# A graph network on one core: the scaled variance ahead of the second half's normalisation, and two buffers of powers

## The reference, cut to what matters

```
m_j = einsum('bnd,do->bno', h, W1[:D])
m_i = einsum('bnd,do->bno', h, W1[D:])
pre = m_j[:, None, :, :] + m_i[:, :, None, :] + b1
msg = gelu(_layernorm(pre, g1, be1), approximate=False)
agg = einsum('bijo,bij->bio', msg, adjacency)
updated = _layernorm(concatenate([h, agg]) @ W2 + b2, g2, be2)
```

## Time and profile before

| | |
|---|---|
| time, median of 3 runs | 4087.21 us (4080.77 to 4090.16) |
| the profiled execution | 4083.3 us, of which the span 4081.4 us |
| granted TensorE clock, mean | 0.923 |
| busy: DVE, PE, ACT, POOL | 83%, 81%, 68%, 52% of the span |
| slot steps | 310, in 16 groups |

### The profile page before, as it was taken

One profiled execution on the slowest core, in us unless ns is written; L12 is line 12 of the kernel. 1 busy time (PEld: TensorE's weight loads), 2 busy tenths in 40 slices (PEclk: granted clock), 3 DMA queues, 4 the chain that ended last, 5 costly groups with the idle time before them and its releaser, 6 DMA issues.

```text
span 4081.4 us, 93269 instructions
## 1 busy us (share of the span) xinstructions
PE 3302.0 (81%) x25274; PEld 2780.7 (68%) x25556; DVE 3378.2 (83%) x12271; ACT 2785.5 (68%) x6381; POOL 2108.6 (52%) x1923
## 2 busy tenths in 40 slices
PE   3484688887888888888798888888887887988898
PEld 2273567677676777767677776767776676776777
DVE  4788888898888888888888888888898888887830
ACT  2484676858667586776858676685868768595753
POOL 1182663718547292753729274471827547192730
PEclk7596899989899999999999999999999999999999
DMA  2000001000010100001010000101000010000000
GB/s 81 26 1 26 1 1 42 1 22 21 1 43 1 43 0 22 22 1 43 1 35 9 22 22 1 43 1 43 0 22 22 1 43 1 27 0 1 16 1 21
DMA packets 95513, 73.89 MB, mean 18 GB/s; under 512 B 7504, under 2 KB 95184, under 8 KB 95184
## 3 DMA queue, kind: packets, MB, share of 16 engines
q1 hardware_dynamic: 95184, 70.09, 5.7%
HBM read 61.68 MB, written 8.39 MB: 17 GB/s over the span
## 4 chain that ended last, share of the span: by engine, by line
issue 26%; POOL 25%; DVE 21%; PE 16%; ACT 6%; DVEq 3%; POOLq 2%; ACTq 0%; DMA 0%; SPq 0%
POOL v_z L511 18%; POOL v_diag L517 3%; PE n_bank_d L1599 3%; PE n_bank_d L1600 3%; PE n_bank_c L1582 3%; DVE v_normed L971 2%; PE n_bank_d L1596 2%; POOL v_prstd L525 2%; DVE v_top_at L1043 2%; PE n_bank_b L1660 1%; DVE v_top L1040 1%; PE n_bank_d L1496 1%; ACT v_pair L842 1%; DVE v_adj_x L1048 1%; POOLq L532 1%
## 5 line engine op out<-in xcount | busy, mean ns | idle before, releaser
L511 POOL TENSOR_TENSOR v_z<-v_z,all_bc_L_gnn_be 128x512 f32<-128x512 f32 x620 | 786.2, 1269 | 22.0 <-DVE v_z L1093 22.0
L525 POOL TENSOR_TENSOR v_prstd<-v_pvar,all_neg_half 128x8 f32<-128x8 f32 x310 | 563.5, 1818 | 267.8 <-DVE v_pvar L1109 240.0
L1496 PE MATMUL n_bank_d<-v_diag,v_msg 128*128 128x128 f32 x4960 | 637.1, 284 | 32.2 <-ACT v_diag L740 32.2
L1496 PEld LDWEIGHTS n_bank_d<-v_diag,v_msg 128*128 128x128 f32 x4960 | 594.8, 197 | 35.2 <-ACT v_diag L740 35.2
L740 ACT ACTIVATE v_diag<-all_ident,v_value 128x128 f32<-128x128 f32 x1860 | 572.5, 386 | 0.0
L1485 PE MATMUL n_bank_b<-v_parts,v_onehot 128*128 128x128 f16 x5472 | 374.0, 224 | 152.6 <-ACT n_bank_b L682 152.6
L1485 PEld LDWEIGHTS n_bank_b<-v_parts,v_onehot 128*128 128x128 f16 x5472 | 332.7, 100 | 224.7 <-ACT n_bank_b L682 183.5
L1582 PE MATMUL n_bank_c<-all_l_wsd,v_fT 128*128 128x256 f32 x1792 | 449.1, 392 | 31.4 <-ACT v_adjT L667 28.9
L1485 PE MATMUL n_bank_c<-v_parts,v_onehot 128*128 128x128 f16 x4960 | 346.9, 226 | 141.7 <-ACT n_bank_c L682 141.6
L1485 PEld LDWEIGHTS n_bank_c<-v_parts,v_onehot 128*128 128x128 f16 x4960 | 308.6, 101 | 213.2 <-ACT n_bank_c L682 168.4
L677 ACT ACTIVATE v_fT<-n_bank_d,all_l_c 128x256 f32<-128x256 f32 x256 | 119.7, 474 | 447.1 <-PE n_bank_d L1600 446.9
(11 more groups left out here) (281 smaller groups left out, 7344.6 us busy)
## 6 DMA issues: line engine op xcount, KB each, us to landing
v_adj_l<-in_adj SPq DMA_DIRECT2D x128, 256.0 KB, 3.7
v_adj_x<-in_adj SPq DMA_DIRECT2D x64, 256.0 KB, 3.4
v_ring<-in_x SPq DMA_DIRECT2D x16, 512.0 KB, 5.9
out_x<-v_xout SPq DMA_DIRECT2D x64, 128.0 KB, 2.0
w_wu<-in_L_gnn_wu SPq DMA_DIRECT2D x4, 192.0 KB, 2.5
all_W<-in_L_gnn_W SPq DMA_DIRECT2D x2, 128.0 KB, 4.3
w_raw<-in_L_gnn_ws SPq DMA_DIRECT2D x1, 192.0 KB, 3.0
w_raw<-in_L_gnn_wd SPq DMA_DIRECT2D x1, 192.0 KB, 3.1
```

Of the source, the lines that this page charges most:

```text
L511: nc.gpsimd.tensor_tensor(z[par][:, units], z[par][:, units], wide(bc["L2_gnn_be1"])[:, units], ALU.add).then_inc(sem["z_ready"], 1)
L525: nc.gpsimd.tensor_tensor(prstd[:], pvar[:], minus_half, ALU.pow).then_inc(sem["prstd_ready"], 1)
L1496: ins = nc.tensor.matmul(ps_agg[:, u // NB, (u % NB) * P:(u % NB + 1) * P], msg[par][:, u], diag[par][:, u], start=False, stop=False, skip ...
```

## The change

Two edits. DVE scales the variance (`pvar`) directly behind the statistics of the second half, and the second half's normalise comes behind it. The powers go to one of two buffers, by `par`, so that the next slot's powers may be written while those of the slot before are still read.

```
-        prstd = plan.sb("prstd", [P, UNITS])
+        prstd = plan.sb("prstd", [P, 2, UNITS])
...
-                    nc.gpsimd.tensor_tensor(prstd[:], pvar[:], minus_half, ALU.pow).then_inc(sem["prstd_ready"], 1)
+                    nc.gpsimd.tensor_tensor(prstd[:, par], pvar[:], minus_half, ALU.pow).then_inc(sem["prstd_ready"], 1)
...
-                        ins = v.scalar_tensor_tensor(z[par][:, u], ps_m[par][:, u], prstd[:, u:u + 1],
+                        ins = v.scalar_tensor_tensor(z[par][:, u], ps_m[par][:, u], prstd[:, par, u:u + 1],
...
                         ins.then_inc(sem["stats_done"], 1)
-                        if not first:
+                        if half_ == 0 and not first:
                             dve.wait_ge(sem["prstd_ready"], step + 1)
-                            dve.wait_ge(sem["msg_ready"], step * 2 + (half_ + 1))
-                            normalise(1 - par, half_)
+                            dve.wait_ge(sem["msg_ready"], step * 2 + 1)
+                            normalise(1 - par, 0)
                     dve.wait_ge(sem["stats_done"], step * 2 + 2)
                     v.tensor_scalar(pvar[:].rearrange("p (q u) -> p q u", u=2), pstats[:, par, :, :, 2], 1.0 / D, UP * UP * LN_EPS,
                                     ALU.mult, ALU.add).then_inc(sem["pvar_ready"], 1)
+                    if not first:
+                        dve.wait_ge(sem["msg_ready"], step * 2 + 2)
+                        normalise(1 - par, 1)
                     pick(dve.snap(step + g * 2 + 2), par)
```

## The result

The changed kernel takes 4122.7 us (median of 4, 4121.5 to 4123.9) against 4086.0 (4 runs, 4080.8 to 4090.2): ratio 1.009, 95% interval 1.0075 to 1.0105. Forecast were 4096 us and 4066 to 4112: a loss of 9 us, where it is 37.

What follows compares the result with a forecast made beforehand. POOL's own work and a loop through DVE's `pvar` were taken as tied at 5.11 us a step. The profiled 4083.3 us plus 16 x 0.6 = 9.6 gave 4093; from the median 4087.2, about 4096 us, range 4066 to 4112.

Steps and rivals of the forecast that it cites:

- parts (a) to (d): Steady step: `pvar` moves 1.03 us earlier, is held by POOL's shift; the loop through ScalarE gives 5.10 us, from 5.11.
- Three signs: `pvar` mean 0.7 to 0.9 us; powers 1.65 to 1.75 us; shift at a group's end waits about 0.6 us.
- part (e): Group's end, 16 times: later second-half normalise and gather make POOL's shift 0.6 us later; 9.6 us in all.
- the first steps: Start of a group: powers of step 3 come 0.05 to 0.1 us sooner, the last powers 0.2 us sooner.
- Rival 4: Slot phase: later gathers in first steps delay the 2.4 GHz clock, or a loop term grows; 13 to 16 us more; chance 0.12.
- it is 0.6 us later, and with it the next mix: Group's end: the late shift delays the next mix by as much, nothing covers it; 16 x 0.6 is 9.6 us.

Runs made afterwards that it cites:

- x5: Kernel before, its order kept, with `pvar` as a TENSOR_REDUCE instead of a TENSOR_SCALAR: 4071.6 us, ratio 0.9949.
- x6: Changed kernel with `pvar` as a TENSOR_REDUCE instead of a TENSOR_SCALAR: 4057.3 us, ratio 0.9906.
- x12: Changed kernel with TENSOR_REDUCE `pvar`, no wait for the last gather, matmuls of zeros in the mix and each group's second step: 3986.3 us, ratio 0.9741.
- x2: Kernel before, its order kept, with six unused normalisations ahead of a group's last eight to make its end late: 4129.4 us, ratio 1.009.
- x4: Changed kernel with ten matmuls of zeros in TensorE's 2.61 us wait in the mix: 4091.9 us, ratio 1.000.
- x3: Changed kernel without VectorE's wait for a group's last gather: 4118.5 us, ratio 1.0064.

## Why the prediction came out wrong

**Right: parts (a) to (d).** `pvar` arrives in the shift and is held to its end (0.68 us, ends 0.04 behind the shift); the powers don't hold DVE; the loop is that of the second-half normalise, ScalarE and the gather, and the step is 5.096 us over the later steps, 5.10 forecast. Of the 1.03 us moved 0.015 a step is kept. x5 and x6 show the hold by taking it away. Three signs were off in size: the mean of `pvar` is 0.62 us (0.7 to 0.9 forecast), the powers are recorded with 1.78 (1.65 to 1.75), and the shift at a group's end waits 1.11 for DVE (0.6). One reading was loose: the TENSOR_SCALAR at 342.89 ends 0.28 us behind POOL's instruction, not with it; nothing rests on the difference.

**Right in kind, 0.17 us short: part (e).** Forecast from powers to shift were 4.54 us (1997.32 to 2001.86), measured 4.71 in the group shown. The term that is off is the one from the last second-half normalise to its gather: 2.21 forecast, 2.39 measured. The row it came from has 2.24 (1996.07 to 1998.31), so 0.03 was lost there for no stated reason. The 0.15 left is ScalarE's: the last gather starts 1.98 us behind its first seed before and 1.97 after (1996.33 and 2008.57 for the seeds), but that seed now comes 0.42 behind the second-half normalise, as ScalarE is still at its gelu, where it was 0.26. The other two, 1.28 and 1.21, measured 1.28 and 1.20. As a mean over the groups the end grew by 0.92 (14.8 over 16), where it was to be 0.8.

**Wrong: the first steps.** With the fourth powers 0.05 to 0.1 us sooner, and the steps behind them, a group's last powers were to come 0.2 us sooner, 3.2 in all. Measured is 0.8 later in all (+1.9, -1.1). The first two steps do better than I had followed: 4.60 and 4.93, 0.65 less than before. The third gives 0.76 back. PE's timeline of these steps, with ScalarE's second seed of the second step, before and in the changed kernel:

```profile
1903.88 1.89 PE L1485 MATMUL n_bank_b<-v_parts,v_onehot 128*128 128x128 f16 x16 [3.00 <-ACT n_bank_b L682]
...
1909.79 1.89 PE L1485 MATMUL n_bank_c<-v_parts,v_onehot 128*128 128x128 f16 x16 [1.46 <-ACT n_bank_c L682]
...
1912.32 1.44 PE L1485 MATMUL n_bank_c<-v_parts,v_onehot 128*128 128x128 f16 x16
...
1904.92 0.60 ACT L682 ACTIVATE n_bank_b<-v_own 128x512 f32<-128x512 f32 x1 [1.09 <-DVE v_z L1093]
```

```profile
1914.48 1.07 PE L1488 MATMUL n_bank_b<-v_parts,v_onehot 128*128 128x128 f16 x16 [2.85 <-ACT n_bank_b L682]
...
1921.10 1.89 PE L1488 MATMUL n_bank_c<-v_parts,v_onehot 128*128 128x128 f16 x16 [3.14 <-ACT n_bank_c L682]
...
1923.63 1.91 PE L1488 MATMUL n_bank_c<-v_parts,v_onehot 128*128 128x128 f16 x16
...
1916.23 0.60 ACT L682 ACTIVATE n_bank_b<-v_own 128x512 f32<-128x512 f32 x1 [1.81 <-DVE v_z L1093]
```

The gathers into bank c start 10.50 us behind the group's first powers (1910.60), where before it was 9.79 (1900.00). These 0.71 us are the hold: ScalarE's second seed waits for the second-half normalise, which stands behind the held `pvar`, and follows the first seed by 2.41 us where it was 1.70. Every group has the shift of 0.7 us, and in x6, where nothing is held, it is 0.2. The clock comes on top. In the group shown the bank c gathers take 1.89 and 1.91 us at 1.2 GHz; before they took 1.89 and 1.44, so they were mostly at the low level too, while the gather of 1903.88 was at 1.2 GHz before and that of 1914.48 is at 2.4 GHz now. There the low stretch has moved back rather than come new. Rival 4 names this second part; what the low level costs in all is seen where the waits are filled, in x12.

**Wrong, and the step that failed: "it is 0.6 us later, and with it the next mix".** I took the mix as a block that shifts without changing its length. It grew by 2.3 us in each middle one and by 22.1 over all, more than half of the loss. The parts of the miss: 22.1 for the mixes, 4.0 for the first steps and those behind them (0.8 against -3.2), and some 2 for the end add up to 28, and the profiled executions differ by 28.6 more than the 9.6 forecast. Rival 4 came nearest, with a chance of 0.12: it had the right mechanism, the granted clock, but looked for it only in the slot phase. For the mix I took no cost from the clock, though the windows view of before grants 0.94 from 1997 to 2141 us, about what the slot phase has. x2 shows that a start one microsecond late is enough for the growth, x4 that the clock carries it.

**Open.** What sets the level behind the 2.61 us wait. Both kernels have both levels. In before the nine middle mixes have the high one, but the mixes behind the second, third and fourth group the low one; here is the fourth:

```profile
1110.56 0.75 PE L1448 MATMUL n_bank_a<-all_ident,v_adj_l 128*128 128x128 f32 x4 [2.61 <-ACT v_adjT L642]
1111.10 1.10 PE L1596 MATMUL n_bank_d<-v_fT,all_l_wn 128*128 128x256 f32 x2
```

That mix takes 136.51 us at a granted clock of 0.90, like those of the changed kernel (136.30 for the same one). In the changed kernel the mix behind the second group has the high level, and it is 1.7 us shorter than in before. A late start is enough to bring the low level (x2) and is not needed for it: x3, whose ends are early, and x5, whose ends lie as before, have it too. No run shows what decides, nor which shift would have spared the mixes.

## What to carry to other kernels

When a change shifts the work behind it by even a microsecond, do not take the stage behind it as a block: cut both traces at the same instructions, compare the stretches, and where one has grown, look for a TensorE wait with matmuls at half speed behind it, and fill that wait with matmuls of zeros as a test. A small VectorE instruction that others wait for should be of a kind that GpSimd doesn't hold, here a TENSOR_REDUCE; only then did moving it forward win anything, and an order that measures as nothing can be worth 1% once the hold is gone.

## What was not expected of the hardware

- Of two kernels with the same 2.61 us wait ahead of the same matmuls, one has them at 2.4 GHz and the other four pairs of them at 1.2 GHz (0.59 and 1.06 us); the 1.6 us that this adds reach DVE whole, by way of ACT. An end 1 us late brought mixes up to 2.5 us longer (x2).
- Twenty-four matmuls of zeros a group, 5.5 us of TensorE's time, made the kernel 17 us faster.
- The powers are recorded with 1.78 us in the changed kernel, but the next shift starts 1.61 behind their start, inside that record. Counted to the next shift's start, as a mean over 294 steps, the powers take 1.79 us in before and 1.80 in x5, where a compare is under way when they start, and 1.62 in the changed kernel and in x6, where it starts 0.87 and some 0.5 us into them and costs nothing.
- A TENSOR_REDUCE of 128x16 takes 0.17 us inside a running GpSimd shift, where a TENSOR_SCALAR of half the elements takes until the shift's end.
